# A recommender tower on one core: look-ups sent in runs of three, three and two behind memsets, and one early look-up made to wait

## The chip, the core and the metric

The kernel runs on one core of a Trainium2 chip, in one launch. The metric is the device time of the whole execution in microseconds, the median of several runs. TensorE (PE) multiplies matrices, VectorE (DVE) and ScalarE (ACT) work element by element, GpSimd (POOL) here issues table look-ups, and SyncE (SP) issues the other transfers. The engines run their own instruction streams side by side and tell each other how far they are through semaphores: an instruction may wait until a semaphore has reached a number, and an instruction that ends may raise one.

## What is computed

1024 samples have 32 fields each. A field is an index into its own table of 64-wide rows. Every pair of the 32 fields (496 pairs) has its own 64x64 matrix; its interaction is one number for each sample. These 496 numbers and 16 dense features go through a three-layer network.

```python
e = jnp.stack([tbl_0[ids[:, 0]], tbl_1[ids[:, 1]], ...], axis=1)      # 1024 x 32 x 64
p, q = e[:, ROW], e[:, COL]                                           # ROW, COL: the 496 pairs
z = jnp.sum(jnp.einsum('bpj,ipj->bpi', p, K) * q, axis=-1)            # 1024 x 496
h = jnp.concatenate([z, dense_ctx], axis=1)                           # 1024 x 512
h = jnp.maximum(h @ W_top1 + b_top1, 0.0)
h = jnp.maximum(h @ W_top2 + b_top2, 0.0)
y = h @ W_top3
```

## The kernel before

**Tiling.** The samples are taken in 4 blocks of 256 (`SIZE`), the fields in 16 pairs. A *tile* is two fields of one block, so there are 64 of them, numbered m = 0 to 63 in the order of `tile_at(m)`. Three tiles of the first block (m = 0, 1 and 4, `BY_PRODUCT`) come from small tables and are made by products of TensorE with one-hot matrices `ones` (L664), which DVE (L594) and ACT (L527, L531) build. Each of the other 61 is fetched by four *look-ups* of GpSimd (L417): an indirect DMA that takes 128 rows of 64 numbers out of a table, by a column of `ids_sb`, into the buffer `nat`. That makes 244 look-ups, issued strictly in order.

**What happens to a tile.** When its four look-ups have landed, TensorE transposes it (L642, raising `transposed`) into the PSUM tile `t_ps`, and ACT copies it into `rows` (L490; L488 for products that lie in `z_ps`). From the 17th tile on (m = 16) tiles are transposed two at a time.

**Pieces, sums and groups.** TensorE's main work is 248 *pieces*: 192 doubles (L688, L695) and 56 passes (L709). Each fills one of three PSUM banks `u_ps` (`URING`) and raises `u_ready`. DVE multiplies the bank by embeddings (L605, L608, L616) and raises `prod_ready`, which frees the bank for the piece three later. TensorE then sums the products of two doubles into `z_ps` (a *quad*: L722, L728, raising `summed`), and ACT sums those of a pass (L502). Quads stand behind every second double. A *group* is what lies from one place with quads to the next, two or three pieces.

**What sets the order.** The class `Plan` fixes the order of TensorE's pieces, transpositions and quads in advance, by assumed costs; all engines follow it. GpSimd's waits are these:

- a tile's first look-up waits until the tile eight earlier is transposed (`transposed >= m - LANES + 1`, `LANES` = `RING` = 8), as it takes its buffer; the first eight tiles wait for none. So the stream begins with 17 look-ups with no wait but that for the indices (the four of tiles 2, 3, 5 and 6 and the first of tile 7);
- each later look-up waits for the number of pieces and quads that `PLAN.in_front(m, part)` gives. These numbers spread the look-ups evenly over TensorE's work. At tile 16 they are 32, 34, 34 and 35 pieces, at tile 61 they are 206, 207, 209 and 209, at tile 63 214, 215, 217 and 217. Tiles 60 and 61 are transposed behind piece 213, tiles 62 and 63 behind piece 221 (pieces count from 0).

The loads of the matrices `k_sb` on SP wait for `transposed` too. After the last piece the network's three layers follow (L769, L789 and later), without look-ups.

Of the kernel before, what the change touches and what calls it, by code (L numbers as in the profile page):

```python
# [8 lines left out]
P = 128  # L9
# [64 lines left out]
URING, PRING, CRING, RING, LANES = 3, 8, 3, 8, 8  # L74
# [29 lines left out]
def tile_at(m):  # L104
    b, tile = divmod(m, TILES)
    return b, FRONT[tile] if b == 0 and tile < len(FRONT) else tile
# [16 lines left out]
def lane_count(m):  # L123

    return 32 * SUBS * (m // LANES + (m % LANES not in BY_PRODUCT))
# [2 lines left out]


AHEAD = 30  # L130


def pieces_in_front(m):
    return max(0, (4 * m - AHEAD) * (ND + NP) // (4 * TILES))

# [9 lines left out]
class Plan:  # L145
# [90 lines left out]
    def in_front(self, m, part):  # L236

        first, last = (next(mark[0] for mark in self.marks if mark[1] == n * (ND + NP)) for n in (1, BLOCKS))
        due = first + (last - first) / (4 * (LOOKED_UP - TILES)) * (4 * (m - TILES) - AHEAD + part)
        return max(mark for mark in self.marks if mark[0] <= max(0, due))  # L240
# [45 lines left out]
PLAN = Plan()  # L286
AT = {what: n for n, what in enumerate(PLAN.order)}
PIECES = len(PLAN.order)
SELFS = [(b, d) for b, d, _ in PLAN.order if d is not None and DOUBLES[d][1] is None]
assert PIECES == len(AT) == BLOCKS * (ND + NP) and PLAN.folds == BLOCKS  # L290


def tower(nc, ids, first_ids, tables, kern, dense, w1, b1, w2, b2, w3, out):
    f32, f32r, u32 = mybir.dt.float32, mybir.dt.float32r, mybir.dt.uint32
    ALU, ACT = mybir.AluOpType, mybir.ActivationFunctionType
    with ExitStack() as ctx:
        def sb(name, shape, dt=f32):
            return ctx.enter_context(nc.sbuf_tensor(name, shape, dt))
# [4 lines left out]
        def sem(name):  # L303
            return ctx.enter_context(nc.semaphore(name))
# [2 lines left out]
        rows = sb("rows", [P, TILES, BATCH])  # L307
        nat = sb("nat", [P, RING, SUBS, P])
        nat01 = sb("nat01", [P, 2, SUBS, 2, P])
        prod = sb("prod", [P, PRING, 2, 2, SIZE])  # L310

        with nc.sbuf_tensor("id_row", [1, 2 * SIZE * PRODUCTS], f32r) as id_row, nc.sbuf_tensor("one_row", [1, PART], f32r) as one_row:
# [56 lines left out]
        small_ids_in, small_table_in = sem("small_ids_in"), [sem(f"small_table_in{t}") for t in range(PRODUCTS)]  # L369
        one_line_ready, one_row_ready, ids_copied, id_row_ready, ids_spread = sem("one_line_ready"), sem("one_row_ready"), sem("ids_copied"), sem("id_row_ready"), sem("ids_spread")  # L370
        sel_zero, sel_ready = sem("sel_zero"), sem("sel_ready")
        gathered = [sem(f"gathered{s}") for s in range(LANES)]
        transposed, rows_ready, by_self_in = sem("transposed"), sem("rows_ready"), sem("by_self_in")
        k_in = [sem(f"k_in{n}") for n in range(TILES)]
        u_ready, prod_ready, summed, z_out = sem("u_ready"), sem("prod_ready"), sem("summed"), sem("z_out")
# [6 lines left out]
        def nat_of(m, s):  # L382

            b, tile = tile_at(m)
            return nat01[:, b % 2, s, tile, :] if tile < 2 else nat[:, m % RING, s, :]
# [5 lines left out]
        @block.gpsimd  # L391
        def _(pool):
            nc.gpsimd.memset(ident[:], 0.0).then_inc(ident_zero, 1)
            pool.wait_ge(ident_zero, 1)
            nc.gpsimd.affine_select(out=ident[:], in_=ident[:], compare_op=ALU.not_equal, fill=1.0, base=0,
                                    pattern=[[-1, P]], channel_multiplier=1).then_inc(ident_ready, 1)
            nc.gpsimd.iota(row_number[:], [[1, CHUNKS]], base=0, channel_multiplier=CHUNKS,
                           allow_small_or_imprecise_dtypes=True).then_inc(row_number_ready, 1)
            pool.wait_ge(ids_in, 16)
            for m in range(LOOKED_UP):  # L400
                if m in BY_PRODUCT:
                    continue
                b, tile = tile_at(m)
                if m >= LANES:
                    pool.wait_ge(transposed, m - LANES + 1)
                if tile == 0 and b >= 2:
                    pool.wait_ge(prod_ready, AT[b - 2, None, NP - 1] + 1)
                for n in range(SUBS):
                    for h in range(2):
                        _, pieces, quads = PLAN.in_front(m, 2 * n + h)  # L410
                        if pieces:
                            pool.wait_ge(u_ready, pieces)
                        if quads:
                            pool.wait_ge(summed, quads)
                        f = 2 * tile + h
                        col = (b * SUBS + n) * FIELDS + f
                        pool.indirect_dma_start(  # L417
                            nat_of(m, n)[:, h * EMBED:(h + 1) * EMBED], None, tables[f],
                            bass.IndirectOffsetOnAxis(ids_sb[:, col:col + 1], 0)).then_inc(gathered[m % LANES], 16)
            for m in range(LOOKED_UP - LANES, LOOKED_UP):  # L420
                pool.wait_ge(gathered[m % LANES], lane_count(m))

        @block.sync
        def _(sp):
# [12 lines left out]
            def by_self_load(n):  # L437

                b, d = SELFS[n]
                tile = DOUBLES[d][0]  # L440
                sp.wait_ge(rows_ready, b * TILES + tile + 1)
                if n > 0:
                    sp.wait_ge(prod_ready, AT[SELFS[n - 1] + (None,)] + 1)
                for bank in range(2):
# [127 lines left out]
        def _(dve):  # L572
# [23 lines left out]
            def multiply_double(n, b, d):  # L596
# [9 lines left out]
                else:  # L606
                    dve.wait_ge(by_self_in, 64 * (SELFS.index((b, d)) + 1))
                    nc.vector.tensor_tensor(to, u, by_self.rearrange("p s b n -> p b s n"), ALU.mult).then_inc(prod_ready, 1)  # L608
# [16 lines left out]
        def _(pe):  # L625
# [148 lines left out]
            pe.wait_ge(zT_out, BLOCKS - 2)  # L774
            pe.wait_ge(prod_ready, PIECES)
            for n in range(4):
# [73 lines left out]
```

## Time and profile before

| | before |
|---|---|
| median of 3 runs | 493.63 us (490.99 to 494.14) |
| profiled execution, its own time | 490.83 us |
| its span, first to last instruction | 489.1 us |
| PE busy | 445.8 us, 91% |
| DVE busy | 303.2 us, 62% |
| ACT busy | 260.7 us, 53% |
| POOL busy | 232.3 us, 48% |
| chain that ended last, by engine | PE 82%, another core or an unknown queue 6%, DVE 6% |
| mean granted TensorE clock | 0.972 |

The profile is of one execution. Its rows say for each instruction when it started, how long it took, how long its engine had been idle before it, and what ended that idle time ("issue": nothing that the profile shows; "remote": a semaphore whose raiser the profile can't name). Instructions that only wait or raise a semaphore have no rows. The profiled execution lies at the lower end of the runs, 0.6% below their median.

### The profile page before, as it was taken

The numbers are of one execution on the slowest core, as the hardware profiler recorded it, in microseconds if no ns is written. First come the engines' busy times: TensorE is split into PE (matmuls) and PEld (weight loads), VectorE is DVE, ScalarE is ACT, GpSimd is POOL, SyncE is SP. The second block draws the span as 40 slices with busy tenths as digits, with TensorE's granted clock in tenths as the row PEclk, the third lists the DMA queues.
The fourth block names the chain that finished last, engine by engine and source line by source line (L and its number), as shares of the span: only waits on it lengthen the run. The fifth ranks groups of instructions, "written<-read, shape, count | busy, mean of one in ns | idle before, by whom it ended". The sixth has DMA issues, their size and how long they took to land.

```text
span 489.1 us, 10184 instructions
## 1 busy us (share of the span) xinstructions
PE 445.8 (91%) x3421; PEld 249.8 (51%) x3421; DVE 303.2 (62%) x293; ACT 260.7 (53%) x1874; POOL 232.3 (48%) x251
## 2 busy tenths in 40 slices
PE   8469989989998999799998998899999899999997
PEld 4136545545555455355654554555554555564443
DVE  7316567776766677677656775776776878771000
ACT  6026674756656767663566657545586668101122
POOL 6715656566555565556555555556655640000000
PEclk9759999989999999999999999899999999999999
DMA  6145654121018111211121112111121101000000
GB/s 170 42 135 159 195 163 121 21 66 21 19 21 193 23 24 21 66 21 23 20 64 23 25 20 68 20 20 22 24 63 24 21 20 45 0 3 0 0 1 1
DMA packets 18266, 24.31 MB, mean 50 GB/s; under 512 B 6387, under 2 KB 11767, under 8 KB 17958
## 3 DMA queue, kind: packets, MB, share of 16 engines
q1 hardware_dynamic: 10406, 15.64, 10.9%
q0 software_dynamic: 7808, 8.01, 8.4%
q8 instruction: 28, 0.46, 0.4%
q14 instruction: 24, 0.20, 0.1%
HBM read 19.44 MB, written 0.00 MB: 40 GB/s over the span
## 4 chain that ended last, share of the span: by engine, by line
PE 82%; another core or an unknown queue 6%; DVE 6%; issue 3%; ACT 2%; POOL 0%; POOLq 0%; DVEq 0%; ACTq 0%
PE u_ps L688 36%; PE u_ps L709 13%; PE z_ps L722 11%; PE u_ps L769 6%; PE z_ps L728 6%; DVE prod L605 5%; PE t_ps L642 4%; PE u_ps L789 3%; PE u_ps L695 1%; PE z_ps L664 1%; DVE prod L608 1%; DVE pass_prod L616 0%; PE u_ps L631 0%; ACT prod L522 0%
## 5 line engine op out<-in xcount | busy, mean ns | idle before, releaser
L417 POOL DMA_INDIRECT nat<-tbl,ids_sb x244 | 231.2, 947 | 166.7 <-issue 59.0
L605 DVE TENSOR_TENSOR prod<-u_ps,rows 128x1024 f32<-128x1024 f32 x184 | 218.2, 1220 | 106.8 <-PE u_ps L688 53.3
L502 ACT ACTIVATE pass_prod<-pass_prod 128x64 f32<-128x64 f32 x896 | 214.6, 243 | 38.0 <-DVE pass_prod L616 30.4
L688 PE MATMUL u_ps<-rows,k_sb 64*128 64x256 f32 x1472 | 194.3, 395 | 16.6 <-DVE prod L605 9.3
L688 PEld LDWEIGHTS u_ps<-rows,k_sb 64*128 64x128 f32 x1472 | 133.3, 187 | 102.8 <-issue 46.4
L502 ACT ACTIVATION_READ_ACCUMULATOR pass_prod<-pass_prod 128x1 f32 x896 | 169.5, 189 | 3.6 <-issue 3.6
L616 DVE TENSOR_TENSOR pass_prod<-u_ps,nat 128x1024 f32<-128x1024 f32 x56 | 68.1, 1217 | 23.9 <-PE u_ps L709 19.0
L709 PE MATMUL u_ps<-k_sb,rows 64*128 64x256 f32 x448 | 65.1, 408 | 5.7 <-DVE prod L605 3.5
L722 PE MATMUL z_ps<-prod,sel 128*32 128x512 f32 x512 | 69.9, 612 | 0.0
L490 ACT ACTIVATE rows<-t_ps 128x512 f32<-128x512 f32 (+1 forms) x38 | 19.5, 514 | 90.0 <-remote 55.3
L709 PEld LDWEIGHTS u_ps<-k_sb,rows 64*128 64x128 f32 x448 | 43.0, 194 | 22.9 <-DVE prod L605 8.3
L728 PE MATMUL z_ps<-prod,sel 128*32 128x256 f32 x512 | 37.1, 385 | 1.4 <-issue 1.3
L769 PE MATMUL u_ps<-zT,rows 128*128 128x512 f32 x64 | 27.7, 594 | 0.0
L642 PE MATMUL t_ps<-ident,nat 128*128 128x128 f32 x122 | 22.2, 298 | 3.9 <-issue 3.0
L728 PEld LDWEIGHTS z_ps<-prod,sel 128*32 128x32 f32 x512 | 14.4, 109 | 18.5 <-issue 12.0
L642 PEld LDWEIGHTS t_ps<-ident,nat 128*128 128x128 f32 x122 | 13.1, 145 | 17.6 <-issue 17.6
L722 PEld LDWEIGHTS z_ps<-prod,sel 128*32 128x32 f32 x512 | 10.4, 109 | 18.8 <-issue 16.0
L769 PEld LDWEIGHTS u_ps<-zT,rows 128*128 128x128 f32 x64 | 12.1, 190 | 15.2 <-issue 15.2
L560 ACT ACTIVATE k_sb<-u_ps,b_sb 128x512 f32<-128x512 f32 x8 | 5.5, 687 | 22.4 <-PE u_ps L769 22.4
L511 ACT ACTIVATE zT<-z_ps 128x256 f32<-128x256 f32 x4 | 1.5, 384 | 29.8 <-PE z_ps L728 23.6
L664 PE MATMUL z_ps<-zT,rows 125*64 125x256 f32 x16 | 6.5, 538 | 8.8 <-issue 7.7
L789 PE MATMUL u_ps<-k_sb,rows 128*128 128x512 f32 x32 | 13.9, 592 | 0.0
(50 smaller groups left out, 95.8 us busy)
## 6 DMA issues: line engine op xcount, KB each, us to landing
by_self<-rows SPq DMA_DIRECT2D x32, 128.0 KB
nat<-tbl,ids_sb POOLq DMA_INDIRECT x244
k_sb<-kern SPq DMA_DIRECT2D x3, 768.0 KB
k_sb<-kern SPq DMA_DIRECT2D x2, 640.0 KB
k_sb<-kern SPq DMA_DIRECT2D x1, 1152.0 KB
k_sb<-kern SPq DMA_DIRECT2D x2, 512.0 KB
rows<-w SPq DMA_DIRECT2D x1, 1024.0 KB
rows<-tbl SPq DMA_DIRECT2D x4, 224.0 KB
```

The source lines that it names most:

```text
L417: pool.indirect_dma_start(nat_of(m, n)[:, h * EMBED:(h + 1) * EMBED], None, tables[f], bass.IndirectOffsetOnAxis(ids_sb[:, col:col + 1], 0 ...
L490: nc.scalar.activation(rows[:, tile:tile + count, cols_of(b)], t_ps[:, 0:count].rearrange("p t n c -> p t (n c)"), ACT.Copy).then_inc(rows ...
L502: op = nc.scalar.activation(of, of, ACT.Copy, accum_out=z_nat[:, b % 2, s, row:row + 1])
L605: nc.vector.tensor_tensor(to, u, by.unsqueeze(1).to_broadcast([P, 2, 2, SIZE]), ALU.mult).then_inc(prod_ready, 1)
L616: nc.vector.tensor_tensor(pass_prod[:, k % CRING], u, by.to_broadcast([P, 2, 2, SIZE]), ALU.mult).then_inc(prod_ready, 1)
L642: op = nc.tensor.transpose(t_ps[:, t, s, :], nat_of(m + t, s), ident[:])
L688: op = nc.tensor.matmul(u[:, h, :], k_sb[part, k_of(d), side, :], rows[part, tile, cols_of(b)], start=True, stop=True)
L709: op = nc.tensor.matmul(u_ps[:, n % URING, h, t, :], rows[part, first + t, at:at + P], k_sb[part, k].rearrange("p s n -> p (s n)"), start= ...
L722: op = nc.tensor.matmul(z_ps[32 * k:32 * k + 32, :, :], sel[:, 30 - 2 * slot:62 - 2 * slot], prod[:, (a + k // 2) % PRING, k % 2], start=s ...
L728: op = nc.tensor.matmul(z_ps[32 * k:32 * k + 32, 0, :], sel[:, 30 - row:62 - row], prod[:, (a + k // 2) % PRING, k % 2, side], start=slot ...
L769: op = nc.tensor.matmul(h_ps(n), w1_sb[:, r * (HID1 // P) + m, :], zT[:, r, cols], start=r == 0, stop=r == ZROWS - 1)
L789: op = nc.tensor.matmul(h_ps(8 + n), w2_sb[:, g * (HID2 // P) + m, :], h1T(g, cols), start=g == 0, stop=g == HID1 // P - 1)
```

## The change

All of it is on GpSimd.

- `IN_STEP = {5: 4}`: tile 5's first look-up, which waited for nothing, waits until four tiles are transposed (m = 0 to 3: the products 0 and 1 and the looked-up tiles 2 and 3). Everything behind it on GpSimd waits with it.
- From tile 16 (`RUNS_FROM`) on, the waits for pieces and quads of each single look-up are dropped. Look-ups are counted in eights (two tiles); at the first, fourth and seventh of the eight a run begins, so the runs are three, three and two long. Ahead of each run stand two (`PAUSE`) memsets of a new tile `zeros` (128x128), each followed by a wait on its own semaphore `zeros_there`, and then one wait for `u_ready`: three runs to three groups, each waiting for all pieces but the last one of its group (`GROUP_ENDS`). There are 72 runs, so 144 memsets and 72 waits for pieces stand where 192 look-ups had a wait each.
- The waits for `transposed` and for `prod_ready` stay. TensorE's, DVE's, ACT's and SP's streams are the same.

The numbers that the runs wait for, beside those of before: tile 16 33, 33, 33, 35 (before 32, 34, 34, 35); tile 61 208, 208, 211, 211 (206, 207, 209, 209); tile 63 216, 216, 219, 219 (214, 215, 217, 217).

```diff
+IN_STEP = {5: 4}
+RUNS_FROM, RUNS, PAUSE = 16, (0, 3, 6), 2
...
+GROUP_ENDS = [n for n, quads in enumerate(PLAN.quads) if len(quads)]
+FIRST_GROUP = next(g for g, n in enumerate(GROUP_ENDS) if n >= PLAN.in_front(RUNS_FROM, 0)[1])
...
+        zeros = sb("zeros", [P, P])
...
+        zeros_there = sem("zeros_there")
...
+            pauses = 0
             for m in range(LOOKED_UP):
...
-                if m >= LANES:
+                if m in IN_STEP:
+                    pool.wait_ge(transposed, IN_STEP[m])
+                elif m >= LANES:
                     pool.wait_ge(transposed, m - LANES + 1)
...
                         _, pieces, quads = PLAN.in_front(m, 2 * n + h)
-                        if pieces:
+                        if pieces and m < RUNS_FROM:
                             pool.wait_ge(u_ready, pieces)
-                        if quads:
+                        if quads and m < RUNS_FROM:
                             pool.wait_ge(summed, quads)
+                        if m >= RUNS_FROM:
+                            three_groups, place = divmod(4 * (m - RUNS_FROM) + 2 * n + h, 8)
+                            if place in RUNS:
+                                for _ in range(PAUSE):
+                                    pauses += 1
+                                    nc.gpsimd.memset(zeros[:], 0.0).then_inc(zeros_there, 1)
+                                    pool.wait_ge(zeros_there, pauses)
+                                pool.wait_ge(u_ready, GROUP_ENDS[FIRST_GROUP + 3 * three_groups + RUNS.index(place)])
```

GpSimd's stream at the start, before: the last three look-ups of the second fetched tile (tables 2 and 3) and the first of tile 5 (tables 10 and 11). The names are output, table, indices, and the shape.

```order
L417 DMA nat01<-tbl_3,ids_sb 128x64
L417 DMA nat01<-tbl_2,ids_sb 128x64
L417 DMA nat01<-tbl_3,ids_sb 128x64
L417 DMA nat<-tbl_10,ids_sb 128x64
L417 DMA nat<-tbl_11,ids_sb 128x64
L417 DMA nat<-tbl_10,ids_sb 128x64
```

The same place after (the line number is now 434):

```order
L434 DMA nat01<-tbl_3,ids_sb 128x64
L434 DMA nat01<-tbl_2,ids_sb 128x64
L434 DMA nat01<-tbl_3,ids_sb 128x64
L434 DMA nat<-tbl_10,ids_sb 128x64 [waits transposed]
L434 DMA nat<-tbl_11,ids_sb 128x64
L434 DMA nat<-tbl_10,ids_sb 128x64
```

No look-up moved against another, but the first 17 are cut into 8 and 9 by a wait.

GpSimd's stream at the 17th and 18th tile (m = 16 and 17, tables 0 to 3 of the second block), before:

```order
L417 DMA nat01<-tbl_0,ids_sb 128x64 [waits summed,u_ready,transposed]
L417 DMA nat01<-tbl_1,ids_sb 128x64 [waits summed,u_ready]
L417 DMA nat01<-tbl_0,ids_sb 128x64 [waits summed,u_ready]
L417 DMA nat01<-tbl_1,ids_sb 128x64 [waits summed,u_ready]
L417 DMA nat01<-tbl_2,ids_sb 128x64 [waits summed,u_ready,transposed]
L417 DMA nat01<-tbl_3,ids_sb 128x64 [waits summed,u_ready]
L417 DMA nat01<-tbl_2,ids_sb 128x64 [waits summed,u_ready]
```

The same place after, to the first look-up of the third run:

```order
L429 MEMSET zeros 128x128 [waits transposed]
L429 MEMSET zeros 128x128 [waits zeros_there]
L434 DMA nat01<-tbl_0,ids_sb 128x64 [waits u_ready,zeros_there]
L434 DMA nat01<-tbl_1,ids_sb 128x64
L434 DMA nat01<-tbl_0,ids_sb 128x64
L429 MEMSET zeros 128x128
L429 MEMSET zeros 128x128 [waits zeros_there]
L434 DMA nat01<-tbl_1,ids_sb 128x64 [waits u_ready,zeros_there]
L434 DMA nat01<-tbl_2,ids_sb 128x64 [waits transposed]
L434 DMA nat01<-tbl_3,ids_sb 128x64
L429 MEMSET zeros 128x128
L429 MEMSET zeros 128x128 [waits zeros_there]
```

Where each look-up had its own wait for pieces, a run has one, with two memsets ahead of it; the wait of the second tile for its buffer (`transposed`) now lies inside a run.

## Rows read from the trace of the kernel before

**Rows 1.** The page: busy us, share and instructions; busy tenths of 16 DMA engines.
```profile
PE 445.8 (91%) x3421; PEld 249.8 (51%) x3421; DVE 303.2 (62%) x293; ACT 260.7 (53%) x1874; POOL 232.3 (48%) x251
...
DMA  6145654121018111211121112111121101000000
```

**Rows 2.** The page's costliest groups: busy us, mean ns of one, idle before, releaser.
```profile
L605 DVE TENSOR_TENSOR prod<-u_ps,rows 128x1024 f32<-128x1024 f32 x184 | 218.2, 1220 | 106.8 <-PE u_ps L688 53.3
```

**Rows 3.** The windows: busy us (and instructions) while tiles 16 to 63 are looked up.
```profile
core 0: us, PE busy (x) PEld busy (x) DVE busy (x) ACT busy (x) POOL busy (x), PEclk, DMA share, GB/s
88.50:404.50 316.00, 291.81 (x2444) 167.41 (x2442) 222.93 (x191) 194.77 (x1490) 182.86 (x194) 0.98 0.17 37
```

**Rows 4.** The timeline from 249 us: start us, duration us, instruction [idle before <-releaser].
```profile
249.17 2.00 PE L688 MATMUL u_ps<-rows,k_sb 64*128 64x256 f32 x16
...
251.00 1.03 PE L709 MATMUL u_ps<-k_sb,rows 64*128 64x256 f32 x8
...
251.13 0.95 POOL L417 DMA_INDIRECT nat<-tbl,ids_sb  x1 [0.30 <-issue]
...
253.20 2.36 DVE L605 TENSOR_TENSOR prod<-u_ps,rows 128x1024 f32<-128x1024 f32 x2 [3.01 <-PE u_ps L709]
...
253.93 0.95 POOL L417 DMA_INDIRECT nat<-tbl,ids_sb  x1 [1.85 <-PE z_ps L728]
```

**Rows 5.** The chain that ended last, 420 to 445 us, after all look-ups.
```profile
424.25 1.93 PE u_ps L688 x16
426.18 1.00 PE z_ps L728 x16
427.18 1.93 PE u_ps L688 x16
```

**Rows 6.** The timeline of ACT, first 46 us.
```profile
27.56 0.38 ACT L490 ACTIVATE rows<-t_ps 128x256 f32<-128x256 f32 x1 [15.98 <-remote]
...
31.59 0.38 ACT L490 ACTIVATE rows<-t_ps 128x256 f32<-128x256 f32 x1 [0.84 <-PE t_ps L642]
38.74 0.39 ACT L488 ACTIVATE rows<-z_ps 128x256 f32<-128x256 f32 x1 [6.76 <-PE z_ps L664]
```

**Rows 7.** The timeline of POOL, first 46 us.
```profile
0.74 0.20 POOL L393 MEMSET ident<- 128x128 f32 x1 [0.29 <-POOLq L806]
1.19 0.64 POOL L395 TENSOR_SCALAR_AFFINE_SELECT ident<-ident 128x128 f32<-128x128 f32 x1 [0.24 <-POOL ident L393]
...
12.21 0.95 POOL L417 DMA_INDIRECT nat<-tbl,ids_sb  x1 [0.31 <-issue]
...
23.47 0.95 POOL L417 DMA_INDIRECT nat<-tbl,ids_sb  x1 [0.30 <-issue]
34.47 0.95 POOL L417 DMA_INDIRECT nat<-tbl,ids_sb  x1 [10.05 <-PE u_ps L709]
```

**Rows 8.** The timeline of POOL at tiles 16 to 63: starts of runs.
```profile
90.36 0.95 POOL L417 DMA_INDIRECT nat<-tbl,ids_sb  x1 [0.30 <-issue]
92.58 0.94 POOL L417 DMA_INDIRECT nat<-tbl,ids_sb  x1 [1.27 <-remote]
...
97.78 0.95 POOL L417 DMA_INDIRECT nat<-tbl,ids_sb  x1 [1.75 <-PE u_ps L688]
...
169.79 0.95 POOL L417 DMA_INDIRECT nat<-tbl,ids_sb  x1 [0.47 <-issue]
...
173.06 0.95 POOL L417 DMA_INDIRECT nat<-tbl,ids_sb  x1 [1.08 <-PE u_ps L709]
...
373.93 0.95 POOL L417 DMA_INDIRECT nat<-tbl,ids_sb  x1 [1.00 <-PE u_ps L688]
...
376.80 0.95 POOL L417 DMA_INDIRECT nat<-tbl,ids_sb  x1 [0.67 <-issue]
...
392.91 0.95 POOL L417 DMA_INDIRECT nat<-tbl,ids_sb  x1 [1.13 <-PE z_ps L722]
...
397.58 0.94 POOL L417 DMA_INDIRECT nat<-tbl,ids_sb  x1 [1.23 <-PE u_ps L688]
398.83 0.95 POOL L417 DMA_INDIRECT nat<-tbl,ids_sb  x1 [0.30 <-issue]
```

**Rows 9.** The timeline from 322.1 us: a tile's last look-up and its transposition.
```profile
322.16 0.95 POOL L417 DMA_INDIRECT nat<-tbl,ids_sb  x1 [0.30 <-issue]
...
324.69 0.41 PE L642 MATMUL t_ps<-ident,nat 128*128 128x128 f32 x2 [0.54 <-issue]
```

## Prediction

> **What bounds the kernel now.** I read the page's busy times first. TensorE is busy for 445.8 of 489.1 us, no other engine for more than 62% [rows 1]: the time is TensorE's work plus what it stands. Then I read where it stands. While tiles 16 to 63 are looked up, TensorE is busy for 291.81 of 316.00 us, so it stands for 24.2, and DVE, which frees TensorE's banks, is idle for 316.00 - 222.93 = 93 us [rows 3]. DVE's main line has idle time of 106.8 us in all, most of it ended by TensorE's pieces [rows 2]. After the look-ups nothing of this is left: in the chain of waits a group of two doubles and a quad repeats every 427.18 - 424.25 = 2.93 us, 1.93 of doubles and 1.00 of quad, with no gap [rows 5].
>
> Why does DVE wait for pieces that are done? The timeline around 250 us shows it. Two doubles ran from 249.17 to 251.17 and a pass to 252.03, so the first double was done at about 250.2. DVE had been idle for 3.01 us when it began on it at 253.20. In between GpSimd was issuing look-ups back to back; the last ran from 251.13 to 252.08 [rows 4]. So TensorE's message arrived 253.20 - 251.13 = 2.07 us after the last look-up of a run began, 1.12 after it ended. I read this as: while look-ups follow each other at 1.25 us, messages from TensorE to others are held up, and they come through when the run ends.
>
> The same at the start, larger. ACT stands for 15.98 us and copies the first product's tile at 27.56, 4.09 us after the last of 17 look-ups in a row began at 23.47 [rows 6, 7].
>
> **Tile 5's wait.** It leaves eight look-ups in the first run; the last still begins at 12.21 [rows 7]. Its messages come through between 12.21 + 2.07 = 14.3 (as at 250 us) and 12.21 + 4.09 = 16.3 (as at 27.56); I take the middle, 15.3, since eight lie between the four and the seventeen. From ACT's first copy to its copy of the fourth tile, which answers to the wait's number, 31.59 - 27.56 = 4.0 us pass now [rows 6]. So tile 5's look-ups start at 19.3 (18.3 to 20.3). Nine go back to back, the last 8 x 1.25 = 10.0 later, at 29.3 (28.3 to 30.3). They hold up messages again, until 2.1 to 4.1 later: 32.4 in the middle, with ends of 30.4 and 34.4. The third product, for which TensorE needs only what DVE and ACT send, is done by then, so ACT's copy of it, now at 38.74 [rows 6], comes at 32.4. That is a gain of 6.3 us, between 4.3 and 8.3. If the second run holds nothing up, the whole front moves with the first message: 27.56 - 14.3 = 13.3 us. If the hold-up is none of the look-ups' doing, the gain is nothing. What hides the wait itself: tile 5's data would be there at about 19.3 + 3.75 + 2.5 = 25.6 (landing below), before TensorE wants it. Behind the waiting look-up stand the rest of tiles 5 to 7; the next look-ups, at 34.47 now, wait for pieces [rows 7], which come earlier too. The DMA engines, at 0.6 in the fullest slices there [rows 1], leave room for the loads behind them.
>
> **Runs of three, three and two.** GpSimd's own need for an eight: 8 x 0.95 of look-ups, 5 gaps of 0.30 within runs, and three pauses. A pause has no row; its parts are bounded by the memset of the same shape, 0.20, the 0.24 that an instruction waited for that memset's semaphore, and the gap of 0.30 [rows 7]: 0.30 + 2 x (0.20 + 0.24) = 1.18 (lower, with waits of 0.20 and a first gap of 0.10: 0.90; upper, if a memset takes as long as the 0.64 of the select beside it: 2.06). So 7.60 + 1.50 + 3 x 1.18 = 12.64 us, between 11.8 and 15.3; I take 1.18, the row being the same operation.
>
> Now an eight takes, from the first start at 90.36 to the last at 398.83, 191 steps in 308.47 us [rows 8], 12.92 us. So GpSimd's stream alone would not bind at 1.18. What would is the loop: the next run waits for pieces, whose message is held up by the run before. For that the trace has runs of the same lengths. From a run's start to the next one's, the runs of three took 5.20 (92.58 to 97.78, the first) to 4.67 (392.91 to 397.58, the last), mean 4.88 of 17; the runs of two 3.27 (169.79 to 173.06) to 2.87 (373.93 to 376.80), mean 3.31 of 20 [rows 8]. An eight is then 2 x 4.88 + 3.31 = 13.07 us. The stretch from the first look-up of tile 16 to the last of tile 63 is 23 eights and the last one's two runs of three and one step, 23 x 13.07 + 9.76 + 1.25 = 311.6, against 308.47: a loss of 3.1 us. TensorE's own need, its busy share 291.81/316.00 of 12.92, is 11.93 and doesn't bind. What covers the memsets is this loop: they run while the message is on its way. The cover is gone from a pause of (13.07 - 9.10)/3 = 1.32 on, each 0.1 more costs 0.3 x 24 = 7 us.
>
> By the Trainium skill ("SBUF — State Buffer", section "Who interferes with whom") a DMA never contends with a compute engine. The 3.01 us that DVE stood beside look-ups [rows 4] are no proof against it, as a message is not SBUF data; if nothing but SBUF's ports counted here, cutting look-ups into runs would bring nothing, the fourth rival below.
>
> **The sum**, against the profiled execution's own time of 490.83 (span 489.1 and 1.7 around it): 490.83 - 6.3 + 3.1 = 487.6 us. This execution lies 2.8 us below the median of 493.63, so a run of the same luck as the median would be at 490. I forecast 487.6.
>
> **Rivals.**
>
> 1. *GpSimd runs free.* A run begins on a message that is already there, as only one wait stands for three look-ups and the pause lets messages through. Then DVE's lateness goes and an eight takes what GpSimd (12.64, or 11.8) or TensorE (11.93) needs, say 12.2: 24 x (12.92 - 12.2) = 17 us less, 490.8 - 6.3 - 17 = 467, at 12.64 rather 478. I put it at 473. For it: 93 us of DVE's idle time is there to be won [rows 3]. Against: the runs of three and two of before were begun by a wait each and still took 4.88 and 3.31 [rows 8].
> 2. *The start gives all of its 13.3 us*: 490.8 - 13.3 + 3.1 = 481. For it: the first product needs no look-up. Against: the nine look-ups after the wait fall on the third product.
> 3. *Slower: the eighth's last run comes too late for the transposition.* The two look-ups at places 7 and 8 wait for 211 pieces where they waited for 209, and TensorE transposes both tiles behind piece 213. From piece 210's end there is one piece (0.97), a quad (1.00) and two doubles (1.93) [rows 5]: 3.9 us. The look-ups need a start of about 0.25, 1.25 and the landing, 324.69 - 322.16 = 2.53, at which TensorE already stood for 0.54 [rows 9]: 4.0 us, and whatever the message is late. TensorE then stands L + 0.1 in each eight: 11.93 + L + 0.1. It decides beyond 13.07 from L = 1.0 and costs over 1% from L = 1.4, an eight of 13.4; at the 1.8 to 1.9 that would follow from a message that leaves early in a run, an eight is 13.9: 24 x 0.98 = 23 us, 490.8 - 6.3 + 23 = 508. For it: the tight landing. Against: the run ahead is over by then, which lets the message through after 1.12 [rows 4].
> 4. *The hold-up isn't the look-ups' doing*, so that neither part gives anything: 490.8 + 3.1 = 494.
>
> **How the numbers follow.** Forecast 0.38 (482 to 494: the start's ends of 4.3 and 8.3 and some 0.15 us on an eight either way), rival 1 0.20, rival 2 0.14, rival 3 0.17, rival 4 0.11. A measurement of this kernel can tell about 1%, 4.9 us, from no change. Faster by over that: rival 1, most of rival 2 and those three tenths of the forecast that gain more, 0.20 + 0.13 + 0.11 = 0.44. Slower: most of rival 3 and a little of rival 4, 0.16 + 0.02 = 0.18. Between: 0.38. The range reaches to the middle of rival 1 and leaves out the half of it below, and all but the smaller sizes of rival 3: 473 to 502.
>
> **What would show it.** In the changed kernel's profile: ACT's first copy from `t_ps` at 14 to 16 us and not 27.56; tile 5's first look-up at 18 to 20 with TensorE as releaser; ACT's copy of the third product at 30 to 34. From tile 16 on: memsets of 0.20 us and a pause of 1.2; runs of three that start 4.9 apart; an eight in 13.1 us; DVE's idle time in that stretch still near 90 us. Wrong if the starts of runs show GpSimd never waiting for TensorE (rival 1, or a pause over 1.32), if TensorE stands more than 1 us before each transposition (rival 3), or if ACT's first copy stays near 27 us (rival 4).

## The result: slower by 2%, and the profile after

The changed kernel takes 502.4 us (median of 6 runs, 498.99 to 503.63), the kernel before 492.95 in the same comparison; the ratio is 1.0196, 95% interval [1.0166, 1.0227]. The profiled execution took 503.63 us, its span is 501.8. The forecast was 487.6 us, 473 to 502. Ratios, here and below, leave out executions in a slower state: one of e3 (1939.66 us), one of e9 and one of the kernel before.

TensorE's busy time in the two profiles is nearly the same, 444.9 against 445.8 us [rows 1]. What it stands grew from 489.1 - 445.8 = 43.3 us to 501.8 - 444.9 = 56.9. The page of the kernel after, busy times, and two of its costliest groups (busy, mean ns, idle before, releaser):

```profile
PE 444.9 (89%) x3421; PEld 255.0 (51%) x3421; DVE 301.5 (60%) x293; ACT 260.3 (52%) x1874; POOL 262.6 (52%) x395
...
L659 PE MATMUL t_ps<-ident,nat 128*128 128x128 f32 x122 | 22.4, 301 | 31.0 <-issue 29.3
...
L429 POOL MEMSET zeros<- 128x128 f32 x144 | 30.7, 213 | 4.2
```

The same group of transpositions in the page of the kernel before:

```profile
L642 PE MATMUL t_ps<-ident,nat 128*128 128x128 f32 x122 | 22.2, 298 | 3.9 <-issue 3.0
```

TensorE is now idle for 31.0 us ahead of transpositions, where it was idle for 3.9. The releaser "issue" doesn't say so, but what it waits for there is a tile's last look-up, as one eight shows. The timelines of POOL and PE after, around 271 us (start, duration, instruction, idle before):

```profile
270.61 0.94 POOL L434 DMA_INDIRECT nat<-tbl,ids_sb  x1 [0.30 <-issue]
271.85 0.94 POOL L434 DMA_INDIRECT nat<-tbl,ids_sb  x1 [0.30 <-issue]
272.78 0.49 POOL L429 MEMSET zeros<- 128x128 f32 x2
274.39 0.95 POOL L434 DMA_INDIRECT nat<-tbl,ids_sb  x1 [1.12 <-PE u_ps L705]
275.64 0.95 POOL L434 DMA_INDIRECT nat<-tbl,ids_sb  x1 [0.30 <-issue]
276.59 0.48 POOL L429 MEMSET zeros<- 128x128 f32 x2
277.59 0.95 POOL L434 DMA_INDIRECT nat<-tbl,ids_sb  x1 [0.52 <-issue]
```

```profile
270.03 1.09 PE L712 MATMUL u_ps<-rows,k_sb 64*64 64x256 f32 x16
...
276.06 1.13 PE L726 MATMUL u_ps<-k_sb,rows 64*128 64x256 f32 x8
278.21 0.63 PE L659 MATMUL t_ps<-ident,nat 128*128 128x128 f32 x4 [1.02 <-issue]
```

The eight's last run waits for 140 pieces, the last of which runs from 270.03 to 271.1 (the releaser that the profile names is the piece after it). It begins at 274.39, 3.3 us later: the run ahead of it was issued until 272.79 and held the message up. Its second look-up begins at 275.64, and TensorE, done at 277.2, stands for 1.02 until 278.21. That is 2.57 us after the look-up's start, close to the 2.53 of [rows 9].

Runs and eights. The timeline of POOL after, starts of runs of three and two, near the beginning and at the end of tiles 16 to 63:

```profile
92.43 0.95 POOL L434 DMA_INDIRECT nat<-tbl,ids_sb  x1 [0.52 <-issue]
...
97.51 0.95 POOL L434 DMA_INDIRECT nat<-tbl,ids_sb  x1 [1.16 <-PE u_ps L705]
...
100.71 0.95 POOL L434 DMA_INDIRECT nat<-tbl,ids_sb  x1 [0.52 <-issue]
...
397.09 0.95 POOL L434 DMA_INDIRECT nat<-tbl,ids_sb  x1 [0.52 <-issue]
...
400.83 0.95 POOL L434 DMA_INDIRECT nat<-tbl,ids_sb  x1 [1.06 <-PE u_ps L705]
...
405.96 0.95 POOL L434 DMA_INDIRECT nat<-tbl,ids_sb  x1 [1.20 <-PE u_ps L726]
...
410.40 0.95 POOL L434 DMA_INDIRECT nat<-tbl,ids_sb  x1 [0.52 <-issue]
```

Counted by gaps as in [rows 8], from start to start, a run of three takes 5.08 us early (92.43 to 97.51) and 4.44 late (405.96 to 410.40), mean 5.09 of 45 (the very first is left out); a run of two takes 3.20 (97.51 to 100.71) and 3.74 (397.09 to 400.83), mean 3.39 of 25 (two runs of three that the wait for a buffer broke count here). An eight takes 2 x 5.09 + 3.39 = 13.57 us; before it took 12.92 [rows 8]. Over 24 eights that is 15.6 us more.

TensorE's mean granted clock was 0.956 in this profile and 0.972 in the one before. That does not account for the loss: in f1 below, four runs of the changed kernel had 0.972 in the mean, the runs of the kernel before beside them 0.973, and the ratio was still 1.0158.

The start moved the other way. The timelines of ACT, POOL and DVE after, first 50 us:

```profile
14.77 0.38 ACT L507 ACTIVATE rows<-t_ps 128x256 f32<-128x256 f32 x1 [3.19 <-remote]
...
29.53 0.38 ACT L505 ACTIVATE rows<-z_ps 128x256 f32<-128x256 f32 x1 [10.59 <-remote]
```

```profile
12.15 0.94 POOL L434 DMA_INDIRECT nat<-tbl,ids_sb  x1 [0.30 <-issue]
18.79 0.94 POOL L434 DMA_INDIRECT nat<-tbl,ids_sb  x1 [5.69 <-PE t_ps L659]
...
32.52 0.94 POOL L434 DMA_INDIRECT nat<-tbl,ids_sb  x1 [0.30 <-issue]
36.62 0.94 POOL L434 DMA_INDIRECT nat<-tbl,ids_sb  x1 [3.16 <-remote]
```

```profile
21.05 1.23 DVE L633 TENSOR_TENSOR pass_prod<-u_ps,nat 128x1024 f32<-128x1024 f32 x1 [4.96 <-PE u_ps L726]
35.88 2.36 DVE L622 TENSOR_TENSOR prod<-u_ps,rows 128x1024 f32<-128x1024 f32 x2 [13.60 <-PE u_ps L726]
```

ACT's first copy stands at 14.77 where it stood at 27.56, and its copy of the third product at 29.53, not 38.74 [rows 6]. But the second run is twelve look-ups long, from 18.79 to 33.46, and DVE stands for 13.60 us until 35.88.

### The profile page after: what moved, and what is told of

It is laid out like the page before. It is cut to its first block, busy times and chain, and to the rows that moved or that the text cites. A ratio compares the mean times of both kernels' runs of the same rounds, so it can differ in the third digit from the quotient of the medians.

```text
span 501.8 us, 10208 instructions
## 1 busy us (share of the span) xinstructions
PE 444.9 (89%) x3421; PEld 255.0 (51%) x3421; DVE 301.5 (60%) x293; ACT 260.3 (52%) x1874; POOL 262.6 (52%) x395
## 4 chain that ended last, share of the span: by engine, by line
PE 77%; issue 8%; DVE 6%; another core or an unknown queue 5%; ACT 2%; POOL 1%; DMA 0%; DVEq 0%; POOLq 0%; ACTq 0%
PE u_ps L705 36%; PE u_ps L726 11%; PE z_ps L739 11%; PE u_ps L786 6%; PE z_ps L745 4%; DVE prod L622 4%; PE t_ps L659 3%; PE u_ps L806 3%; PE u_ps L712 1%; PE z_ps L681 1%; POOL nat L434 1%; DVE prod L625 1%; DVE pass_prod L633 1%; DMA nat<-tbl,ids_sb 0%
## 5 line engine op out<-in xcount | busy, mean ns | idle before, releaser
L705 PE MATMUL u_ps<-rows,k_sb 64*128 64x256 f32 x1472 | 200.3, 408 | 13.9 <-DVE prod L622 10.3
L705 PEld LDWEIGHTS u_ps<-rows,k_sb 64*128 64x128 f32 x1472 | 139.6, 196 | 101.6 <-issue 45.0
L739 PE MATMUL z_ps<-prod,sel 128*32 128x512 f32 x512 | 71.1, 628 | 0.0
L726 PE MATMUL u_ps<-k_sb,rows 64*128 64x256 f32 x448 | 63.8, 401 | 5.0 <-DVE prod L622 3.6
L429 POOL MEMSET zeros<- 128x128 f32 x144 | 30.7, 213 | 4.2
```

Source lines behind the costliest of these rows:

```text
L429: nc.gpsimd.memset(zeros[:], 0.0).then_inc(zeros_there, 1)
L705: op = nc.tensor.matmul(u[:, h, :], k_sb[part, k_of(d), side, :], rows[part, tile, cols_of(b)], start=True, stop=True)
L726: op = nc.tensor.matmul(u_ps[:, n % URING, h, t, :], rows[part, first + t, at:at + P], k_sb[part, k].rearrange("p s n -> p (s n)"), start= ...
L739: op = nc.tensor.matmul(z_ps[32 * k:32 * k + 32, :, :], sel[:, 30 - 2 * slot:62 - 2 * slot], prod[:, (a + k // 2) % PRING, k % 2], start=s ...
```

## Experiments

Ratios are to the kernel before, run beside each on the same chip. That kernel took 492.3 to 493.1 us in three of the four comparisons and 485.8 in the one that holds e9 to e12, so times of that one are not set beside the others. Where a time of one comparison is subtracted from that of another, the kernel before differs by up to 0.8 us between them. "Idle before transpositions" is the third number of the group of `t_ps<-ident,nat` as shown above.

### The two parts apart: e1 and e2

e1, the kernel before with tile 5's wait alone:

```diff
+IN_STEP = {5: 4}
...
-                if m >= LANES:
+                if m in IN_STEP:
+                    pool.wait_ge(transposed, IN_STEP[m])
+                elif m >= LANES:
```

> The kernel before with tile 5's wait alone. Theory (the start's gain is real, and what is lost is lost from tile 16 on): in the changed kernel the pieces 34 to 104 lie 2 to 4 us ahead of the kernel before, so this one ends 3.5 us sooner, a ratio of 0.993, and ACT's first copy from t_ps stands near 14.8 us. Rival (the wait itself costs, the later stages lose it again): 1.000 or more.

488.81 us, ratio 0.9916 [0.9886, 0.9946]. The wait gains 3.7 us; the theory's 3.5 was close. This kernel beats both.

e2, the changed kernel with `IN_STEP = {}`:

> The changed kernel without tile 5's wait, so the runs alone. If the two parts simply add up: 502.4 + 3.5 = 506, 13 us over the kernel before, a ratio of 1.027, with TensorE idle for some 30 us before transpositions as in the changed kernel (31.0). If the early look-ups' shift is what brings the runs out of step, it stays within 1% of the kernel before.

506.83 us, ratio 1.0267 [1.0200, 1.0335], idle before transpositions 26.6 us. The runs alone lose 14.3 us. With -3.7 that makes 503.1 against the 502.4 measured: the parts add up, and the whole loss comes with the runs.

### The wait's place and the pauses: e3 to e7

e3, without memsets: `PAUSE` = 0. e4, memsets kept, each run waiting for two pieces fewer (for tile 61 the 209 of before; for most tiles fewer than before, as shown below under "Why the prediction was wrong"):

```diff
-                                pool.wait_ge(u_ready, GROUP_ENDS[FIRST_GROUP + 3 * three_groups + RUNS.index(place)])
+                                pool.wait_ge(u_ready, GROUP_ENDS[FIRST_GROUP + 3 * three_groups + RUNS.index(place)] - 2)
```

> The changed kernel without memsets: runs of three, three and two, each behind its one wait for pieces. Theory A (the last run of an eight waits for pieces too near to the transposition): most runs still start on a message, so only those that started on the pause's end gain, a third of 72 by 0.5 to 0.7 us at most, and TensorE still stands for over 20 us before transpositions: 492 to 502 us. Theory B (the pauses make GpSimd's stream too long: an eight is 9.1 us and three pauses of 1.0 to 1.7): the eights get back 3 x 0.7 us, 17 in all would be more than is lost, so about 487 us with TensorE no longer standing before transpositions.

> The changed kernel, memsets and all, with each run waiting for two pieces fewer (a tile's last look-ups wait for 209 and not 211, as before). Theory A (the wait stands too near to the transposition): TensorE's 31 us before transpositions fall below 8, the 16 us lost from tile 16 on come back for the most part: 486 to 492 us, below the kernel before by the start's gain of 3.5. Theory B (the pauses make GpSimd's stream too long): as before the change of the wait, 500 us or more, as GpSimd can't go faster than its pauses let it.

e3: 496.68 us, 1.0089 [1.0058, 1.0121], idle before transpositions 14.0. e4: 494.92 us, 1.0032 [0.9999, 1.0064], idle 3.5. Each gives back a part, 5.7 and 7.5 us, and e4 brings TensorE's idle time before transpositions back to that of the kernel before, 3.9, with all memsets in place. So theory B of e3, the pauses as the whole cause, falls. Theory A had e3's time right, though not its idle time (over 20 us), and e4's time is 3 to 9 us over what it said.

e5, both at once. e6, five pieces fewer, memsets kept:

> The changed kernel with both mendings: each run waits for two pieces fewer, and no memsets. Theory (the two losses, the waits' place and the pauses, are separate and add up): the four kernels with and without each give 502.4 - 494.9 = 7.5 us for the wait and 502.4 - 496.7 = 5.7 for the pauses, so 489 us, the time of tile 5's wait alone (488.8), with TensorE idle for under 8 us before transpositions. Rival (runs of fixed length cost by themselves, whatever they wait for): 492 to 495 us.

> The changed kernel with memsets, each run waiting for five pieces fewer: nearly two groups, so that a held-up message no longer keeps a run from starting. Theory (then GpSimd's own need and the buffers' release set the runs: 9.1 us and three pauses of 1.0, 12.1 us for an eight, until a look-up waits for its buffer): runs start on the pause's end in most cases, and DVE is late as before, so no more than 2 us either way of 494.9. Rival (GpSimd runs free and messages come through in the pauses): an eight of 12.1 to 12.3 us, 24 x 0.8 = 19 us less than with two fewer, 476 us.

e5: 493.98 us, 0.9996 [0.9946, 1.0046], idle 5.2. e6: 494.71 us, 1.0029 [1.0000, 1.0059], idle 4.3. The losses do not add up: with the early wait the pauses cost 0.9 us, within the noise, with the late one 5.7. So in these four kernels a pause costs clearly only where the last run is already too late. The rival of e5, that runs of fixed length cost by themselves, had the time right: with waits early and no pauses 4 to 5 us are still missing against e1. e6 came out within the 2 us that its theory gave; runs that start earlier gain nothing, and the first rival of the prediction falls.

e5's and e6's profiles show where much of the rest of their loss lies. In e5 ten look-ups follow each other as the runs begin, the last at 93.02. The timeline of DVE in e5:

```profile
90.28 1.23 DVE L622 TENSOR_TENSOR prod<-u_ps,rows 128x1024 f32<-128x1024 f32 x1 [4.57 <-remote]
95.99 1.22 DVE L633 TENSOR_TENSOR pass_prod<-u_ps,nat 128x1024 f32<-128x1024 f32 x1 [4.48 <-remote]
```

DVE stands for 4.57 and 4.48 us, and TensorE's pieces, 3.9 us ahead of the kernel before at the 35th, are 2.8 us behind it at the 40th. After that they lie level with it to 5.6 us behind, and the last is 2.7 behind.

e7, tile 5's wait, no runs, no memsets; from tile 16 on each look-up waits for two pieces more than before:

```diff
                         if pieces:
-                            pool.wait_ge(u_ready, pieces)
+                            pool.wait_ge(u_ready, pieces + 2 * (m >= RUNS_FROM))
```

> The kernel before with tile 5's wait, and from tile 16 on each look-up waits for two pieces more than before: no memsets, no runs of set length. Theory (the wait stands too near to the transposition): TensorE is idle for 12 us or more before transpositions (10.7 with tile 5's wait alone, of which 7 lie in the first 50 us), and the time is 494 to 499 us, 5 to 10 over the 488.8 with tile 5's wait alone. Rival (only the set runs or the memsets lose time): 488 to 491 us.

500.33 us, 1.0139 [1.0090, 1.0187], 11.5 us over e1; idle before transpositions 43.8. Waiting for two pieces more does this without a single memset or set run. The theory holds, and the loss is larger than it said. It is a larger shift than the change made, so its 11.5 us are not the change's share. The group of transpositions in e4 and e7, as above:

```profile
L659 PE MATMUL t_ps<-ident,nat 128*128 128x128 f32 x122 | 22.4, 300 | 3.5 <-issue 2.0 <-ACT rows L507 1.4
```

```profile
L651 PE MATMUL t_ps<-ident,nat 128*128 128x128 f32 x122 | 22.8, 306 | 43.8 <-issue 42.3 <-ACT rows L499 1.6
```

### Which run is too late: e9, e10 and f1 to f4

In e9 only the last run of an eight waits for two pieces fewer (`- 2 * (place == 6)`), in e10 only the first two (`- 2 * (place < 6)`).

> The changed kernel with memsets, where only the last run of each eight (two look-ups) waits for two pieces fewer. Theory (that run alone is too near to the transposition): nearly all of the 7.5 us that all three runs gave come back, 494 to 497 us, and TensorE is idle for under 10 us before transpositions (31.0 in the changed kernel). Rival (the runs ahead hold the last one up as much as its own wait does): 499 us or more, over 20 us idle.

> The counterpart: the first two runs of each eight wait for two pieces fewer, the last one as in the changed kernel. Theory (the last run alone is too near): 500 to 504 us, with TensorE idle for over 20 us before transpositions. Rival (the first two hold the last one up): 494 to 498 us.

e9: 488.14 us, 1.0060 [1.0021, 1.0099], idle 28.3. e10: 491.47 us, 1.0145 [1.0094, 1.0196], idle 16.8. The ratios fit "the last run alone", the idle times contradict it. So the changed kernel (f1), all runs early (f2) and the last run early (f4) were run on one chip, with f3, which is f4 without memsets.

> The changed kernel as it is, as the mark for the three others on the same chip: a ratio of 1.02 to the kernel before, TensorE idle for about 31 us before transpositions. Both theories expect the same of it.

> The changed kernel with two pieces fewer for all three runs, on the same chip: a ratio of 1.003, TensorE idle for under 6 us before transpositions. Both theories expect the same of it.

> Two pieces fewer for the last run of each eight alone, and no memsets. Theory P (with its own wait early, the last run is held by GpSimd's stream, and the pause of 1.0 ahead of it is what makes it late): the last run follows the second at once, 0.7 us sooner, TensorE's idle time before transpositions falls below 10 us, and the ratio is 0.99 to 1.00. Theory W (the waits of the runs ahead hold it up): over 15 us idle, a ratio of 1.005 or more.

> Two pieces fewer for the last run of each eight alone, memsets kept, on the same chip as the changed kernel. Theory O (the last run's own wait is what counts): a ratio of 1.003 to 1.008, and TensorE idle for at most half as long before transpositions as in the changed kernel. Theory G (the last run is then held by the pauses and runs ahead of it): idle for over 20 us, and what the time gains comes from fewer waits for banks.

| | us | ratio | idle before transpositions, us |
|---|---|---|---|
| f1 as changed | 500.36 | 1.0158 [1.0094, 1.0221] | 34.6 |
| f2 all three early | 493.21 | 1.0015 [0.9992, 1.0038] | 4.0 |
| f4 last run early | 504.38 | 1.0245 [1.0172, 1.0318] | 26.4 |
| f3 the same, no memsets | 528.97 | 1.0743 [1.0686, 1.0800] | 5.7 |

Theory O falls: the last run's own wait, moved alone, gains nothing here. G is right about the idle time, but the gain that it put down to fewer waits for banks did not come. In f4 the last run always begins on the pause's end, 1.0 us after the second run, and is nearly as late as before. (In e9, the same kernel on the chip on which everything is quicker, the ratio is 1.0060; the changed kernel was not run there, and why f4 and e9 differ stays open.) Moving all three returns 7.1 us, on one chip.

The idle time fell by 30.6 us from f1 to f2, the time by 7.1. Much of the rest went to another wait. The costliest groups, f1 and then f2:

```profile
L705 PE MATMUL u_ps<-rows,k_sb 64*128 64x256 f32 x1472 | 194.2, 399 | 10.0 <-DVE prod L622 5.4 <-DVE prod L625 2.8 <-issue 1.4
...
L659 PE MATMUL t_ps<-ident,nat 128*128 128x128 f32 x122 | 21.8, 294 | 34.6 <-issue 30.3 <-ACT rows L505 3.1 <-ACT rows L507 1.2
```

```profile
L705 PE MATMUL u_ps<-rows,k_sb 64*128 64x256 f32 x1472 | 194.2, 396 | 24.8 <-DVE prod L622 17.6 <-issue 5.3 <-DVE prod L625 1.6
...
L659 PE MATMUL t_ps<-ident,nat 128*128 128x128 f32 x122 | 21.9, 294 | 4.0 <-issue 2.3 <-ACT rows L507 1.6
```

Idle time before doubles, most of it ended by DVE, which frees the banks, rose from 10.0 to 24.8. I read this so: while TensorE waits for a tile, DVE catches up; when TensorE need not wait there, it waits for a bank sooner.

f3 is the surprise. Idle before transpositions fell below 10 us, as P said, and the time rose by 7% where P had no loss; W left such a time open, but not with this idle time. With its wait met and no pause, the last run follows the second at once: the eights fall into runs of five and three. The timelines of POOL and DVE in f3:

```profile
230.99 0.94 POOL L434 DMA_INDIRECT nat<-tbl,ids_sb  x1 [1.08 <-PE u_ps L705]
...
235.98 0.94 POOL L434 DMA_INDIRECT nat<-tbl,ids_sb  x1 [0.30 <-issue]
239.16 0.94 POOL L434 DMA_INDIRECT nat<-tbl,ids_sb  x1 [2.23 <-PE t_ps L659]
...
243.65 0.94 POOL L434 DMA_INDIRECT nat<-tbl,ids_sb  x1 [1.05 <-PE u_ps L726]
```

```profile
234.63 1.23 DVE L622 TENSOR_TENSOR prod<-u_ps,rows 128x1024 f32<-128x1024 f32 x1 [1.53 <-issue]
238.24 4.62 DVE L622 TENSOR_TENSOR prod<-u_ps,rows 128x1024 f32<-128x1024 f32 x4 [2.38 <-PE u_ps L705]
```

An eight takes 243.65 - 230.99 = 12.7 us here and 14.7 in the mean. Four multiplications lie in a row behind the run of five: DVE got the messages of several pieces at once, when the run was over. That the long runs are the cause of the 7% is argued from this place and not shown: of the 26.2 us by which f3's span exceeds f4's (526.8 and 500.6), only 5.9 are idle time of TensorE, and 20.3 are busy time (461.7 and 441.4), at a mean granted clock of 0.948 against 0.969.

### The start once more: e8, and where the waits should stand: e11, e12

e8, e1 with `IN_STEP = {5: 4, 6: 6}`:

> The kernel before with tile 5's wait and one more, tile 6's first look-up behind six transposed tiles, so that the second run is 4 look-ups long and not 12. Theory (what is left of the start's loss is the second run, which held TensorE's messages back from 25 to 35 us): DVE's second piece, at 35.1 with tile 5's wait alone, comes at 27 to 29, and unless the loads of the matrices or the later look-ups take it back, the kernel ends 2 to 6 us sooner, 483 to 487 us. Rival (the look-ups that come later are missed by TensorE): 489 to 493 us.

488.90 us, 0.9915 [0.9887, 0.9943], the same as e1 (488.81). The timeline of DVE in e8:

```profile
25.01 1.23 DVE L608 TENSOR_TENSOR prod<-u_ps,rows 128x1024 f32<-128x1024 f32 x1 [3.46 <-PE u_ps L691]
...
39.40 1.23 DVE L608 TENSOR_TENSOR prod<-u_ps,rows 128x1024 f32<-128x1024 f32 x1 [6.61 <-issue]
44.41 1.23 DVE L608 TENSOR_TENSOR prod<-u_ps,rows 128x1024 f32<-128x1024 f32 x1 [3.78 <-remote]
```

The short second run brings DVE's second piece from 35.1 (e1) to 25.01, as expected, and then DVE stands for 6.61 and 3.78 us. The look-ups that were put off come in one run from 25.85 on. The rival is right in the main: TensorE now stands for a landing, 3.67 us until 32.03, and DVE's stand moves back by a tile.

e11, e1 with two pieces and one quad fewer for each look-up from tile 16 on; e12, the changed kernel without memsets, two pieces fewer from tile 20 on (`- 2 * (m >= 20)`):

> The kernel before with tile 5's wait, where from tile 16 on each look-up waits for two pieces and one quad fewer. Theory (at the old place nothing is left to win before transpositions, and look-ups that may start earlier only follow each other in longer runs, which hold messages up): 489 to 494 us, no gain over the 488.8 with tile 5's wait alone. Rival (the old place is still too late): 484 to 487 us.

> The changed kernel without memsets, each run waiting for two pieces fewer from tile 20 on, but at tiles 16 to 19 as in the changed kernel. With two fewer from tile 16 on, ten look-ups followed each other from 81.6 to 94.0 us and TensorE's pieces 34 to 39 lost 6.5 us there, and next to nothing behind it. Theory (what is left of the loss is that one burst): without it 488 to 490 us, as with tile 5's wait alone. Rival (set runs lose a little everywhere): 492 to 495 us.

e11: 481.14 us, 0.9913 [0.9883, 0.9943]. That is e1's 0.9916: at the old place nothing is left to win by waiting for less. e12: 482.78 us, 0.9969 [0.9930, 1.0008], which on a kernel of 493 us would be 491.5, between the theory's 488 to 490 and the rival's 492 to 495. Inconclusive: six look-ups still followed each other there, up to 94.3 us, and DVE stood for 3.19. How much of what e5 lost is this burst isn't shown.

## Why the prediction was wrong

**What failed** is the step "What would is the loop". It took the spans of runs from the kernel before, 4.88 and 3.31 us [rows 8], and set TensorE's need beside them as a separate bound of 11.93 that "doesn't bind". So it put TensorE's stand for a tile, after the change, at nothing. Those spans were measured where an eight's last look-up begins early enough. From its start to the end of TensorE's work ahead of the transposition, the mean of 24 eights was 4.17 us before and is 2.00 after. The landing takes 2.53 [rows 9]; less than that is left in 3 eights before and in 16 after. TensorE then stands, 25.9 us in all for tiles 16 to 63, and what stands finishes late the pieces on which the next runs wait. The two are one loop, and the forecast took the larger where the stand had to be added. e4, with all waits earlier, has 5.36 us there, runs of 4.80 and 3.52, an eight of 13.12: the forecast's 13.07. The changed kernel has 13.57.

**Why the last look-up is late.** "Two pieces more" is the number of tiles 61 and 63. By `PLAN`, over all eights, the seventh look-up waits for 1.3 pieces more in the mean than before and the eighth for 0.3 more; for the eighth it is two more in 3 eights of 24, none in 11 and one fewer in 4. The larger part, by the starts in the two profiles, is that the eighth has no wait of its own now: it follows the seventh behind one wait and begins 4.04 us after the piece that it waits for, where it was 2.69. No run merges the waits at the old numbers, so no experiment tells the two parts apart. Over the experiments the idle time before transpositions follows the time left: 0.87 us in e7 (idle 43.8), 2.00 in the changed kernel (31.0), 2.29 in f4 (26.4), 3.47 in e3 (14.0), 4.17 before (3.9), 5.36 in e4 (3.5).

**How much of the loss this explains.** Of the 14.3 us that the runs lose (e2), moving all waits gives back 7.1 (f2) to 7.5 (e4). The rest is not settled: e5's rows show a burst of look-ups at tiles 16 to 19, and e12 doesn't tell how much of it that is.

**The third rival was the mechanism**, with a chance of 0.17. Its arithmetic was right for the place that it took, tiles 60 and 61, where three pieces lie between the one waited for and the transposition. Nine eights are like this: TensorE needs 3.8 to 4.1 us there in seven of them, and stands 1.9 in the mean, near the rival's 2.0. But in ten eights four pieces lie between and it stands 0.85, and in five there are more and it doesn't stand. So the price, 508 us, was too high: the rival took the tightest place for all 24, and part of a stand only replaces waits for banks (f1 and f2). The argument against it was wrong: "the run ahead is over by then". In the example above the piece was done at 271.1, the run ahead was issued until 272.79, and the last run began at 274.39; counted so over all 24 eights, it began 2.8 us after its piece, ten times on the pause's end and fourteen on the message. The rival also named only the last run; in f4 its wait alone gained nothing, and in f2 all three gained 7.1 us.

**The start**: the first messages came as said, the size of the gain did not. First copy at 14.77 (forecast 15.3), tile 5's look-up at 18.79 (19.3), TensorE's transposition as its releaser. The gain is 3.7 us (e1), under the 4.3 to 8.3. The step that failed is "Nine go back to back": it was twelve, as the pieces that tile 7's next look-ups wait for were already done, so the second run ended at 33.46 and not at 30.3, and DVE stood until 35.88. Nor is the gain that of the third product's copy, by which it was reckoned: that came 9.2 us sooner, at 29.53 and not 32.4. The second rival, the whole 13.3, falls too: ACT's first copy did move by 12.8 us, but by the 11th piece TensorE is only 3.2 us ahead of the kernel before, and a shorter second run (e8) does not change the time.

**The pause**: forecast 1.18, measured 1.00 where a run begins on its end, as from 276.59 to 277.59; a memset takes 0.213. It lay within the bounds, and GpSimd alone was not the bound, as said. That its cover is gone only beyond 1.32 was wrong: in the changed kernel the memsets cost 5.7 us (e3), where the last run begins 2.8 us after its piece with them and 1.9 without.

**The fourth rival** falls with e1: a wait that cuts the first 17 look-ups gains 3.7 us and moves ACT's first copy by 12.8. By the rule of the Trainium skill ("SBUF — State Buffer", section "Who interferes with whom") that DMA never contends with a compute engine, the cut would bring nothing if only SBUF's ports counted. The 3.7 us show that something else counts too; the rule itself, which is on ports, is not touched by them.

**The range** ended at 502 and the time is 502.4. A time slower by over 1% was given 0.18, though the rows already showed TensorE standing 0.54 us for a landing [rows 9]; it was one of the three tightest eights of the kernel before.

## What to carry to other kernels

Before a wait is moved, or several waits are merged into one, count what has to fit between it and whoever needs the result, at every place and not at one: here three to seven pieces lay between, and the numbers of tile 61 stood for three eights of 24. Two pieces later for every look-up cost 11.5 us by themselves (e7). Where two engines wait for each other in a ring, a span measured in the ring holds only for the waits it was measured with; a stand inside the ring adds to it. An idle time that disappears is not yet a gain: look in the same profile for the wait that took its place (30.6 us went, 7.1 came back).

## What the hardware showed that was not expected

A gap of 1.00 us between runs of look-ups does not always let TensorE's messages through. The timelines of f2 (all three runs early, memsets kept), POOL, PE and DVE:

```profile
88.59 0.95 POOL L434 DMA_INDIRECT nat<-tbl,ids_sb  x1 [0.30 <-issue]
89.54 0.48 POOL L429 MEMSET zeros<- 128x128 f32 x2
90.54 0.95 POOL L434 DMA_INDIRECT nat<-tbl,ids_sb  x1 [0.52 <-issue]
```

```profile
86.41 1.14 PE L705 MATMUL u_ps<-rows,k_sb 64*128 64x256 f32 x8
```

```profile
94.94 4.62 DVE L622 TENSOR_TENSOR prod<-u_ps,rows 128x1024 f32<-128x1024 f32 x4 [4.73 <-remote]
```

The piece that ran from 86.41 was done at 87.6, DVE was free from 90.21 on, and GpSimd issued no look-up from 89.54 to 90.54. DVE began on the piece at 94.94, 0.94 us after the following run was over (94.00). In the same profile a message did come through such a gap. The timelines of POOL and DVE in f2:

```profile
338.84 0.49 POOL L429 MEMSET zeros<- 128x128 f32 x2
339.84 0.95 POOL L434 DMA_INDIRECT nat<-tbl,ids_sb  x1 [0.52 <-issue]
```

```profile
339.74 2.36 DVE L622 TENSOR_TENSOR prod<-u_ps,rows 128x1024 f32<-128x1024 f32 x2 [2.29 <-PE u_ps L705]
```

That piece was done at 337.6, and DVE began on it 0.9 us after the run's end, just before the next look-up. Counted over pieces 36 to 224 of f2, DVE began 35 times at least 1.0 us after its piece was done and after standing for 0.5 or more: 26 times in a longer gap between look-ups, 4 times in a gap of 0.9 to 1.0, 5 times inside a run.

So the memsets do not do what a wait on a message does: a run that begins on a message begins when messages are through, one that begins on the pause's end can prolong the hold-up. By what path the look-ups hold TensorE's messages back is not shown by any run here. Nor is the hold-up complete: in the changed kernel ACT's copy of the third product, released by such a message, began at 29.53, inside the run from 18.79 to 33.46.
